# Two transformer layers on one core: the next batch's first routing made inside the second experts, prefix sums by running totals, first sorted block ahead of the attention run's last values

## The reference, cut to what matters

```
x = x + attention(LN(x)) + experts_top2(LN(x))      # 8 heads, low-rank keys, softmax
x = x + flow_attention(LN(x)) + experts_top4(LN(x)) # 16 heads of width 8, sigmoid
experts_top2: logits = x @ router.T ; best and second best of 8 experts per token,
              out[token] = sum over its two experts e of
                           share_e * ((silu(x @ gate_e.T) * (x @ up_e.T)) @ down_e.T)
experts_top4: four best of 8 experts, weights by a softmax over the four,
              computed here for all tokens and all experts with weight 0 for the rest
```

## Time and profile before

| | |
|---|---|
| median of 3 runs | 2540.83 us (2535.0 to 2545.32) |
| the profiled execution's own time | 2537.11 us |
| its span, first to last instruction | 2535.4 us |
| mean granted TensorE clock | 0.962 |
| scores of the first batch begin at | 49.3 us |
| from a batch to the next | 310 us |

### The profile page before, as it was taken

One profiled execution on the slowest core, in us unless ns is written; L12 is line 12 of the kernel. 1 busy time (PEld: TensorE's weight loads), 2 busy tenths in 40 slices (PEclk: granted clock), 3 DMA queues, 4 the chain that ended last, 5 costly groups with the idle time before them and its releaser, 6 DMA issues.

```text
span 2535.4 us, 64762 instructions
## 1 busy us (share of the span) xinstructions
PE 2310.6 (91%) x25503; PEld 1658.4 (65%) x25503; DVE 1949.4 (77%) x3307; ACT 1660.4 (65%) x3050; POOL 804.1 (32%) x653
## 2 busy tenths in 40 slices
PE   5989989899898998989989899899998999988998
PEld 3667556675666766667657676566665766666765
DVE  6778877788778887687876878868778687786876
ACT  4866558665586656775577755768457684585845
POOL 2221442315324052241522315313253033530334
PEclk8999999999999999999999999999899999999989
DMA  7110221103111121111211112111121102211022
GB/s 252 51 42 2 96 65 43 42 8 116 39 43 42 44 85 35 47 38 45 88 33 48 34 60 77 35 47 31 63 77 36 46 27 76 69 38 48 18 80 63
DMA packets 99123, 141.34 MB, mean 56 GB/s; under 512 B 11523, under 2 KB 60620, under 8 KB 98316
## 3 DMA queue, kind: packets, MB, share of 16 engines
q1 hardware_dynamic: 90636, 120.41, 15.2%
q0 software_dynamic: 8192, 16.79, 2.3%
HBM read 101.84 MB, written 31.13 MB: 52 GB/s over the span
## 4 chain that ended last, share of the span: by engine, by line
PE 72%; DVE 14%; ACT 6%; issue 6%; POOL 1%; SPq 0%; DVEq 0%; DMA 0%; POOLq 0%; ACTq 0%
PE ps L1727 11%; PE ps L1556 11%; PE ps L1749 10%; PE ps L1764 10%; PE ps L1563 6%; PE ps L1638 5%; DVE neg_max L1225 3%; PE ps L1660 3%; PE ps L1513 2%; DVE ffn L1356 2%; ACT probs L833 2%; PE ps L1577 2%; DVE key_low L989 2%; PE ps L1649 1%; PE ps L1850 1%
## 5 line engine op out<-in xcount | busy, mean ns | idle before, releaser
L1225 DVE TENSOR_REDUCE neg_max<-ps 128x1 f32<-128x1024 f32 x512 | 622.8, 1218 | 84.3 <-PE ps L1727 79.0
L833 ACT ACTIVATE probs<-ps,neg_max 128x1024 f32<-128x1024 f32 x512 | 577.3, 1128 | 53.4 <-DVE neg_max L1225 45.7
L1556 PE MATMUL ps<-shared,w_split 128*128 128x512 f32 x1536 | 471.1, 443 | 18.6 <-ACT ffn L884 11.8
L1749 PEld LDWEIGHTS ps<-ident,probs 64*128 64x128 f32 x8192 | 337.5, 144 | 165.0 <-issue 126.3
L718 POOL TENSOR_TENSOR probs<-ffn,shared 128x512 f32<-128x512 f32 x208 | 287.7, 1383 | 415.3 <-DVE ffn L1356 185.5
L1556 PEld LDWEIGHTS ps<-shared,w_split 128*128 128x128 f32 x1536 | 289.3, 193 | 165.9 <-issue 62.4
L1749 PE MATMUL ps<-ident,probs 64*128 64x64 f32 x8192 | 361.4, 230 | 38.1 <-issue 29.6
L884 ACT ACTIVATE ffn<-ps,room_of_gate 128x512 f32<-128x512 f32 x256 | 175.0, 683 | 274.1 <-PE ps L1556 274.1
L1727 PE MATMUL ps<-shared,query_a 64*128 64x512 f32 x1024 | 267.6, 519 | 82.0 <-ACT probs L833 60.1
L1764 PE MATMUL ps<-probsT,latent 128*32 128x128 f32 x8192 | 326.9, 278 | 3.3 <-DVE o_latent L1218 2.3
L817 ACT COPY probsT<-ps 128x512 f32<-128x512 f32 x512 | 303.5, 593 | 24.0 <-PE ps L1749 23.7
(11 more groups left out here) (232 smaller groups left out, 3534.4 us busy)
## 6 DMA issues: line engine op xcount, KB each, us to landing
w_split<-w_parts SPq DMA_DIRECT2D x132, 256.0 KB, 2.6
shared<-gate_rows SPq DMA_DIRECT2D x64, 512.0 KB, 4.4
y_rows<-probs SPq DMA_DIRECT2D x40, 256.0 KB, 2.2
x_in<-in_x SPq DMA_DIRECT2D x9, 512.0 KB, 4.1
out<-x_mid SPq DMA_DIRECT2D x8, 512.0 KB, 3.2
ffn<-in_gate_up SPq DMA_DIRECT2D x1, 2048.0 KB, 8.6
probsT<-in_gate_up SPq DMA_DIRECT2D x1, 2048.0 KB, 13.2
w_down<-in_down SPq DMA_DIRECT2D x2, 1024.0 KB
```

The source lines that it names most:

```text
L833: nc.scalar.activation(probs[:, t % 3, :], banks(2 * (t % 2)), ACT.Exp, bias=neg_max[:, t % 4:t % 4 + 1], accum_out=row_sum[:, g % 2, t % ...
L1225: nc.vector.tensor_reduce(neg_max[:, t % 4:t % 4 + 1], banks(2 * (t % 2)), X, ALU.max, negate=True).then_inc(max_ready.sem, 1)
L1556: mm = nc.tensor.matmul(ps[:, bank, :], w_split[:, f % CHUNK_SLOTS, h, k * P:(k + 1) * P], tokens[:, half], start=(part == 0), stop=(part ...
L1749: mm = nc.tensor.transpose(ps[:, turn_bank(t, c), k * HQ:(k + 1) * HQ], probs[rows, t % 3, k * P:(k + 1) * P], ident[rows, rows])
```

## The change

1. For all batches but the first, `route_two` and `places` no longer run in run 1. DVE makes them in steps 10 to 28 of the second experts of the batch before (`NEXT_ROUTE`, `NEXT_PLACES`: how many pieces at which unit), in the room of `probs` slot 1. PE makes the prefix counts at unit 22. The first batch keeps its routing in run 1.
2. The ranking's two big operations that were POOL's are DVE's, in both places (`ranks`).
3. The prefix counts: DVE makes running totals over the token tiles (`so_far`: one copy and seven sums of 128x8), and PE needs two matmuls where it took nine.
4. `both_on_act` is one tile in eight in run 1 too, so 12 half copies of run 1 move from ACT to DVE (16 were ACT's, 4 stay).
5. POOL scatters at the start of a batch, ahead of `x_mid`, and SP loads `xs` ahead of `x_in`. It waits for the last down product of the batch before.
6. `tokens(0)` with its rounding stands after step 33 of run 1, ahead of step 34 (the last transposes and values), in bank 1. The first block's gate products stand ahead of the values that were in front of them, and the wait for the last copies moves to block 2.
7. Constants of the flow attention: `FLOW_ALLOC` 15 to 17, `FLOW_VALUES` 16 to 18, `NEXT_BETA` 18 to 19, `FLOW_HEADS` 27 to 26, `FLOW_PROJ` 30 to 28. The next heads come one unit earlier for two of the four. The sum of `source_exp` goes to bank 6.

```diff
+TOKENS_STEP = QUAD_STEPS + T_LAG - 2
+NEXT_ROUTE = {10: 2, 17: 1, 18: 2, 19: 1, 20: 2, 22: 4}
+NEXT_PREFIX = 22
+NEXT_PLACES = {22: 1, 24: 4, 25: 2, 26: 4, 28: 4}
...
-NEXT_BETA = 18
+NEXT_BETA = 19
...
-FLOW_ALLOC = 15
-FLOW_VALUES = 16
+FLOW_ALLOC = 17
+FLOW_VALUES = 18
...
-FLOW_HEADS = 27
-FLOW_PROJ = 30
+FLOW_HEADS = 26
+FLOW_PROJ = 28
+NEXT_HEADS = (UNITS - 1, UNITS + 1)
...
 def both_on_act(t):
-    run, i = divmod(t, NT * QUAD)
-    return i % 2 == 0 if run == 0 else i % 8 == 3
+    return t % 8 == 3
...
+                sp.wait_ge(scattered.sem, scattered.at(b, 16 * 2 * NT))
+                sp.sem_inc(rows_complete.sem, 1)
+                if index > 0:
+                    sp.wait_ge(down_done.sem, down_done.at(b, 0))
+                sp.dma_start(xs, x_rows[:, :].rearrange("(j p) d -> p j d", p=P)).then_inc(xs_loaded.sem, 16)
...
-                pool.wait_ge(pairs_made.sem, pairs_made.at(b, 1))
-                nc.gpsimd.tensor_tensor(pair_b, pair_b, earlier[:, :, :].unsqueeze(1).to_broadcast([P, NT, E, E]),
-                                        ALU.mult).then_inc(pairs_step.sem, 1)
-                pool.wait_ge(pairs_step.sem, pairs_step.at(b, 1))
-                nc.gpsimd.tensor_tensor(pair_a, pair_a, pair_b, ALU.add).then_inc(pairs_ready.sem, 1)
...
+                    yield from ranks(logits_first, pairs)
+                    link(nc.vector.tensor_scalar(chosen[:, 0:NT, :], rank[:, :, :], 1.5, None, ALU.is_lt))
+                    link(nc.vector.tensor_copy(so_far[:, 0, :], chosen[:, 0, :]))
+                    for n in range(1, NT):
+                        added = nc.vector.tensor_tensor(so_far[:, n, :], so_far[:, n - 1, :], chosen[:, n, :], ALU.add)
+                        if n < NT - 1:
+                            link(added)
+                        else:
+                            added.then_inc(chosen_ready.sem, 1)
+                        if n % 4 == 3:
+                            yield
...
+                    if index + 1 < BATCH:
+                        if u == min(NEXT_ROUTE):
+                            dve.wait_ge(down_done.sem, down_done.at(b, 1))
+                            dve.wait_ge(rows_stored.sem, rows_stored.at(b, 16))
+                        for _ in range(NEXT_ROUTE.get(u, 0)):
+                            next(next_route, None)
+                        for _ in range(NEXT_PLACES.get(u, 0)):
+                            next(next_place, None)
...
+            def prefixes(made, so_far):
+
+                pe.wait_ge(chosen_ready.sem, chosen_ready.at(made, 1))
+                counts = 2 * P + (NT + 1) * E
+                nc.tensor.matmul(ps[:, 7, 2 * P:counts], before[:, :],
+                                 chosen[:, :, :].rearrange("p n e -> p (n e)"), start=True, stop=False)
+                mm = nc.tensor.matmul(ps[:, 7, 2 * P + E:counts], ones, so_far.rearrange("p n e -> p (n e)"),
+                                      start=False, stop=True)
+                mm.then_inc(prefix_mm.sem, 1)
...
                 for w in range(QUAD_STEPS + T_LAG):
                     attention_step(w)
+                    if w == TOKENS_STEP:
+                        tokens(b, 0)
...
                     if u == FLOW_OUT:
+                        if index + 1 < BATCH:
+                            pe.wait_ge(prefix_taken.sem, prefix_taken.at(b, 1))
```

More of the change, by code:

```diff
@@ L130, in tile_of, with token_bank @@
     return quad * NT * QUAD + s - QUERY_LEAD
+def token_bank(q):
+    return 1 if q == 0 else 2
 def group_at(w, lag):
@@ L840, in attention_step @@
                         copy_xT(b, 0, 0, 2)
-                for w in range(QUAD_STEPS + T_LAG):
-                    attention_step(w)
                 def tokens_high(q):
@@ L1292, in outputs @@
                                           ps[:, 5 + q % 2, 0:len(part) * D]).then_inc(ys_ready.sem, 1)
-                assert next(route, "end") == "end" and next(place, "end") == "end"
+                assert index > 0 or next(route, "end") == "end" and next(place, "end") == "end"
                 for j in range(BLOCKS + BLOCK_DOWN_LAG + 1):
@@ L1766, in values @@
                                              start=(k == 0), stop=(k == NT - 1))
-                    if g == 0 and i == NT // 2 - 1:
-                        pe.wait_ge(chosen_ready.sem, chosen_ready.at(b, 1))
-                        counts = 2 * P + (NT + 1) * E
-                        nc.tensor.matmul(ps[:, 7, 2 * P:counts], before[:, :],
-                                         chosen[:, :, :].rearrange("p n e -> p (n e)"), start=True, stop=False)
-                        for m in range(NT):
-                            mm = nc.tensor.matmul(ps[:, 7, 2 * P + (m + 1) * E:counts], ones,
-                                                  chosen[:, m, :].unsqueeze(1).to_broadcast([P, NT - m, E]),
-                                                  start=False, stop=(m == NT - 1))
-                        mm.then_inc(prefix_mm.sem, 1)
+                    if index == 0 and g == 0 and i == NT // 2 - 1:
+                        prefixes(None, first_so_far)
                     if i == NT // 2 - 1:
```

163 lines of the change are left out of this document (80 added, 83 removed).

## The result

| | before | after |
|---|---|---|
| median | 2539.57 us | 2515.19 us (2512.03 to 2515.78, 4 runs) |
| ratio to before | | 0.9897, 95% interval 0.9879 to 0.9916 |
| profiled execution, its own time | 2537.11 us | 2515.24 us |
| its span | 2535.4 us | 2513.5 us |

(The 2539.57 us are the kernel before beside the changed one. They stand for the 2540.83 us shown above.) The change wins 1.0%, 24 us, where 47 us were forecast. The interval of the ratio stays clear of 1. The time is in the range, but in its upper part, where the rival "The port every time" had put it (2515 us).

What follows compares the result with a forecast made beforehand. PE, busy 91% of the span, was taken as the bound, with gains where it waits or does work that can be left out. The terms were 2537.1 - 42 + 1 - 14.4 + 8.5 = 2490 us, range 2466 to 2522.

Steps and rivals of the forecast that it cites:

- The port every time: Rival, chance 0.15: in the second experts all three places and the small operations wait for POOL in full, 2515 us.
- two rivals at 2515 and 2517 us: DVE waits for POOL in full (chance 0.15, 2515 us); run 1 wins only the prefix counts (chance 0.08, 2517 us).
- Run 1 of batches 2 to 8: Run 1 without routing and prefix counts gets run 2's length: 7 x 5.98 = -42 us, lower end -15.
- of the first, +1: Run 1 of the first batch keeps its routing, DVE becomes the bound at about the old length: +1 us, ends -2 and +5.
- The seam: From run 1's last transposes to the second block's gate products, earlier tokens save 1.8 us in each of 8 batches: -14.4 us.
- The end at which the table load sets the pace: Seam's end of 0 gain, if ACT's table load of 1.28 us and the Silu behind it set the pace.
- The second experts, what goes: PE's stalls of 1.44 us at unit 18 and 1.30 at the beta product can go: 2.74 us in all 8 batches.
- The second experts, what comes: DVE's added work, prefix counts and waits on POOL from unit 17 on: +1.6 us in each of 7 batches, less 2.74 gone.
- the cover of 5.7 us: DVE's idle time up to unit 21, 2.95 us, plus 2.74 us of PE's stalls, against 5.4 us of added work.
- The pair at unit 9: DVE's operation of 1.21 us and POOL's multiplication of 2.18 us, read as in each other's way for their whole length.
- the experts hide everything: Rival, chance 0.15: in the second experts the two stalls go and DVE stays behind PE's pace, -17 us, 2465 us.
- The slower rival: Chance 0.04: DVE becomes the bound of units 17 to 28, 18 us in each of 7 batches, 2605 us.

Runs made afterwards that it cites:

- e7_copies_alone: The kernel before, routing still in run 1, with only the 12 half copies moved from ACT to DVE: 2539.74 us, ratio 0.998.
- e8_tokens_later: The changed kernel with the tokens' product four steps later again, as before the change: 2533.72 us, ratio 0.9973 to the kernel before.
- e6_old_constants: The changed kernel with the flow's allocation, values and beta back at units 15, 16 and 18: 2543.85 us, ratio 1.0007 to the kernel before.
- e1_counts_first: The changed kernel with DVE taking the prefix counts ahead of the four small routing operations at unit 22: 2495.15 us, ratio 0.9833 to the kernel before.
- e2_gate_strip: The changed kernel with POOL multiplying 8 of 512 columns by the gates in units 17 to 28: 2482.25 us, ratio 0.9778 to the kernel before.
- e4_late: The changed kernel with ranking spread one piece to a unit, prefix counts at unit 29, remaining routing and places at the end: 2459.88 us, ratio 0.9691 to before.

## Why the prediction was right or wrong

Forecast were 2490 us, measured are 2515.2: the gain is half of the forecast one. The time lies inside the range because its upper end had been set by two rivals at 2515 and 2517 us. Run 1, the seam and the moved constants came as forecast; what the new work costs the second experts did not.

- **Run 1 of batches 2 to 8, -42, and of the first, +1:** right. The seven batches measure 57.49 to 59.56 us against 58 expected, and the first went from 64.44 to 65.60. In all -41.7 against -41. For the first batch the text had DVE busy for the whole 64.5 us; measured are 61.27 of 65.60. That DVE, as loaded as in run 2, would allow it is what e7_copies_alone shows from the other side: with the routing still there it doesn't. My account of the cause was lopsided, though. I put the 6 us to the counts and ACT's copies; the copies alone gave 0.4 a batch, so the routing's leaving DVE is part of the cause.
- **The seam, -14.4:** right, -15.5. The end at which the table load sets the pace is out by the measured 3.55 us, and e8_tokens_later shows that the early tokens carry the gain.
- **The second experts, what goes, 2.74 a batch:** right in its size. e6_old_constants measures 3.0.
- **The second experts, what comes, +1.6 a batch:** this is the step that failed. The text said: "the ends are 0 and 3.8 and I take about a third, 1.2 us". Measured, the new operations waited 7.8 us in DVE's steps 17 to 22. The three waits on POOL's 512-wide product, priced at up to 1.27 us each, all came (1.07, 1.06 and, on the copy ahead of the totals, 1.12), so a third was the wrong share. Three things more were missed. POOL also has two 1024-wide products there (L743, L738), and an operation that meets one waits up to 1.8 us. The text said that no row of such operations stood at these units, but the trace before has them: a product of DVE's at 331.31 took 2.64 us beside L729. The small operations wait as long as the big ones, the copy with one input too, where I had them in steps 22 to 28 at nothing with an end of 0.9 us. And the cover of 5.7 us was nearly used up by DVE's plain work, 5.4 us, so almost all that came on top went to PE: 7.35 us longer from unit 21 to the out product. The pair at unit 9 was also read loosely. Only POOL's multiplication was prolonged there (2.18 us); DVE's 1.21 us came first.
- **The order in step 22** was not priced at all. The text says of the counts that PE's products "are queued behind them", but not that DVE's copy of the counts stands behind four routing operations while PE's out product waits for it. e1_counts_first gives 16 to 20 us for it. Had I listed what stands ahead of L1146 on DVE, it would have been there in the rows of the order.
- **The clock.** I had counted waits only. A stretch at a low clock came in each batch and cost some 1.5 us of the 6.3. In four of the seven batches it follows the stall ahead of unit 22. In the other three it lies at the flow's first sums, ahead of all these stalls, where the kernel before had it in three of its eight batches too. That the stalls bring it is not shown for those.
- **The rivals.** "The port every time" gave 5.1 us a batch with 2515 us, and it is what happened: the stretch grew by 36.4 us where the rival had 33. That the two are so close is partly luck, since its sum has neither the 1024-wide products nor the order in step 22 nor the clock. I had given it 0.15 and argued against it that DVE may come first. The Trainium skill, page "SBUF — State Buffer", section "Who interferes with whom", says that the two exclude each other and the later one is blocked entirely. The trace agrees: each tensor_tensor in the rows with two inputs in SBUF that began during a product of POOL's waited for its end, and e2_gate_strip shows that the wait goes when POOL's product is cut short. That the experts hide everything is out for this placement, but e4_late shows that more than that can be had: 717.5 us is 24.6 below before. The slower rival, 18 us a batch, was far off.

## What to carry to other kernels

Before putting VectorE work into a stage where GpSimd has a steady product, add to each operation with SBUF inputs the rest of the GpSimd instruction that it will meet, however small the operation is, and hold the sum against the idle time in that stretch (here the reductions were not prolonged). Spread such operations, one piece to a unit, and keep them away from a result that TensorE is about to want. Then ask of every instruction that TensorE waits for what was put ahead of it in VectorE's order: here moving one copy ahead of four small operations gave 16 to 20 us, and one piece to a unit with the rest behind the last dependent unit gave 52 by the ratios (0.9897 against 0.9691), the order in the step included.

## What was not expected of the hardware

- A copy of 128x8 with one SBUF input takes 0.17 us alone and 1.29 us beside GpSimd's product of 1.27 us, which began with it. A conversion of 128x23 (L1179) took 0.76 us instead of 0.18 at 350.13.
- The granted clock fell to 0.50 behind the idle time of 2.67 us in four of the seven batches, and stayed at 1.00 behind the same idle time in the other three. In those it had been low once already, at the flow's first sums (0.63 from 881.03 to 885.00 us in the third batch). What decides between the two isn't shown.
- The load of `x_in` takes 9.7 us to landing where it took 4.1: it now runs at the same time as the scatters. That they slow it was not tested. Nobody waits for it.
